# A four-layer graph network: tile-number tables loaded eight at a time, takes by node tile, four relation buffers, last-source gathers beside a linear layer

## The reference, cut to what matters

```python
h = maximum(layernorm(x), 0); x = x + L0(h)   # three GCN sums: segment_sum(norm * (h @ W)[src], dst)
h = maximum(layernorm(x), 0); x = x + L1(h)   # attention, 4 heads of 8
#   scores = einsum(q[dst], k[src]) / sqrt(8); e = exp(scores - segment_max(scores)[dst])
#   out = (segment_sum(e * v[src], dst) / segment_sum(e, dst)) @ Wo
h = maximum(layernorm(x), 0); x = x + L2(h)   # relational
#   a = tanh(relu(sum((h[src] @ A1 + b) * (h[dst] @ A2 + b + rel_emb[etype])) / sqrt(32)))
#   nei = segment_sum(a * sum_b(w_comp[etype, b] * h[src] @ weight[b]), dst)
#   curr = h[src[last edge of each node]] @ self_loop_weight; out = relu(where(degree > 0, nei + curr, 0))
h = maximum(layernorm(x), 0); x = x + L3(h)   # tensor product
#   message: source features (8 scalars, 8 vectors) times sh0 (1), sh1 (3), sh2 (5) of the edge, mixed; segment_sum by dst
```

## Time and profile before

| | us |
|---|---|
| median of 3 runs | 19102.2 (19086.82 to 19113.71) |
| profiled execution | 19072.43 |
| its span, first to last instruction | 19070.7 |
| records, path, layer 0, tables | 0 to 8208 |
| score pass | 8208 to 10774 |
| softmax, value pass | 10776 to 11757 |
| relation pass | 11935 to 15637 |
| linear layers of layer 2 | 15641 to 15948 |
| harmonic pass | 15989 to 18889 |
| last linear layer, output | 18889 to 19071 |

### The profile page before, as it was taken

The page is one execution under the profiler, slowest core; times in us unless marked ns, Lnnn a source line. Parts: engine busy times, 40 slices in busy tenths (PEclk is TensorE's granted clock), DMA queues, the critical chain, the costliest instruction groups (busy, mean ns, idle before and its releaser), DMA issues. The chain is left out here.

```text
span 19070.7 us, 197183 instructions
## 1 busy us (share of the span) xinstructions
PE 7563.1 (40%) x35336; PEld 4417.5 (23%) x35337; DVE 6411.3 (34%) x15885; ACT 2666.7 (14%) x4339; POOL 9705.1 (51%) x10318
## 2 busy tenths in 40 slices
PE   4122223444441221211111165666666655444445
PEld 1111112222221111110000032233333335322324
DVE  6222222222223333322212465455555532222222
ACT  1121223444441111100000000000000001000001
POOL 0566665555556666556666332444444442555553
PEclk9555556666665555555555555777788865666665
DMA  2111112222211111132222121222222221000001
GB/s 76 28 25 25 25 25 57 58 62 60 60 48 19 19 19 19 19 101 65 64 63 65 41 72 49 52 49 48 49 50 49 50 49 46 18 17 17 17 17 42
DMA packets 756783, 828.62 MB, mean 43 GB/s; under 512 B 348196, under 2 KB 521615, under 8 KB 753650
## 3 DMA queue, kind: packets, MB, share of 16 engines
q0 software_dynamic: 340624, 383.65, 10.8%
q1 hardware_dynamic: 251322, 306.39, 5.2%
q10 hardware_dynamic: 164008, 130.83, 2.5%
HBM read 658.54 MB, written 158.81 MB: 43 GB/s over the span
## 5 line engine op out<-in xcount | busy, mean ns | idle before, releaser
L725 POOL DMA_INDIRECT rel_ring<-scratch_tab,rel_staged x1664 | 1588.0, 954 | 2002.1 <-DVE rel_staged L714 1527.9
L725 POOL DMA_INDIRECT sh_ring<-scratch_tab,sh_staged x1664 | 1569.9, 943 | 1620.1 <-DVE sh_staged L714 1136.1
L664 PE MATMUL rel_accumulator<-rel_message,rel_onehot 128*128 128x512 f32 x3328 | 1930.2, 730 | 808.0 <-issue 488.4
L1186 POOL DMA_INDIRECT sum0g_ring<-scratch_parts,sum0g_staged x1568 | 1540.1, 982 | 1179.7 <-issue 829.7
L1186 POOL DMA_INDIRECT sum1g_ring<-scratch_parts,sum1g_staged x1568 | 1541.7, 983 | 1156.1 <-SPq L1210 653.1
L1818 POOL DMA_INDIRECT score_ring<-scratch_tab,score_staged x1664 | 1583.3, 951 | 1011.8 <-DVE score_staged L714 528.3
L1186 POOL DMA_INDIRECT sum2g_ring<-scratch_parts,sum2g_staged x1568 | 1511.4, 964 | 941.4 <-issue 463.3
L664 PE MATMUL sh_accumulator<-sh_message,sh_onehot 128*128 128x248 f32 x3328 | 1335.0, 555 | 1614.9 <-issue 1380.0
L664 PEld LDWEIGHTS sh_accumulator<-sh_message,sh_onehot 128*128 128x128 f32 x3328 | 850.4, 279 | 2098.9 <-issue 1994.3
L1859 PE MATMUL score_q_edge<-query_parts,score_onehot_t 128*128 x1664 | 422.5, 254 | 2167.5 <-issue 2105.3
L664 PEld LDWEIGHTS rel_accumulator<-rel_message,rel_onehot 128*128 128x128 f32 x3328 | 736.4, 234 | 1696.3 <-issue 1695.5
(11 more groups left out here) (423 smaller groups left out, 12703.9 us busy)
## 6 DMA issues: line engine op xcount, KB each, us to landing
score_rows<-scratch_rel_rows SPq DMA_DIRECT2D x211, 256.0 KB
rel_rel_rows<-scratch_rel_rows ACTq DMA_DIRECT2D x211, 256.0 KB
scratch_kv<-score_ring SPq DMA_DIRECT2D x208, 256.0 KB
value_ring<-scratch_kv SPq DMA_DIRECT2D x208, 256.0 KB, 2.6
rel_type_rows<-scratch_type_rows ACTq DMA_DIRECT2D x211, 172.0 KB
rel_ring<-scratch_tab,rel_staged POOLq DMA_INDIRECT x1672
score_ring<-scratch_tab,score_staged POOLq DMA_INDIRECT x1664
sh_ring<-scratch_tab,sh_staged POOLq DMA_INDIRECT x1664
```

What stands on the lines that cost most here:

```text
L664: last = self.nc.tensor.matmul(into, onehot, part, start=False, stop=True, skip_group_check=True)
L725: nc.gpsimd.indirect_dma_start(out=ring[:, q, g, :], out_offset=None, in_=table, in_offset=bass.IndirectOffsetOnAxis(ap=staged[:, q, g:g + ...
L1186: nc.gpsimd.indirect_dma_start(out=ring[:, q % slots, g, :], out_offset=None, in_=table, in_offset=bass.IndirectOffsetOnAxis(ap=staged[:, ...
```

## The change

- `merge_path` makes two byte tables by step instead of the word of odd bits and the `places` word: `tile_no` (tile number plus one) and `odd`. The word keeps the first tile and the end bits.
- `_eight` loads eight entries of a table into eight registers of TensorE with one call. `_tiles_of` and `_odd_of` use it; `_tile_registers`, `_places` and `Adder` go, and `StepAdder` takes the wait's value and the bank from the tables. The value pass has two banks instead of four and takes tiles in a loop over pairs.
- Relation pass: four buffers for look-up results (PSUM), transposed one-hots and messages; VectorE waits for adds two halves further back, and its order is messages n, staging, logits n+1, one-hots n+4; TensorE looks up half n+4. ScalarE (`_take_ends`) keeps the word, tests a half's four end bits at once and only then each step's bit, and loads the tile number where a tile ends.
- The 98 last-source gathers move to POOL beside `rlo_lin` (`beside`), and `rlo_own` runs after it.
- Harmonic pass: ScalarE only moves finished tiles, in a loop over tiles (`_move_tiles`), and issues the stores of the sums itself; SP loads the factors; VectorE copies them to PSUM, one group ahead.

```diff
+def _eight(nc, engine, table, group, low, high):
+    return nc.values_load_multi_w_load_instructions(
+        table[0:1, bass.ds(group * G, G)], engines=(engine,), min_val=low, max_val=high,
+        skip_runtime_bounds_check_because="a node tile or its place by step")[1]
+def _tiles_of(nc, k, group):
+    return _eight(nc, mybir.EngineType.PE, k["tile_no"], group, 1, JP)
+def _odd_of(nc, k, group):
+    return _eight(nc, mybir.EngineType.PE, k["odd"], group, 0, 1)
...
+class StepAdder:
...
     def add(self, g, onehot, rows):
...
+        if g % 2 == 0:
+            self.pe.wait_ge(self.cleared, self.tiles[g + 1])
+        self.nc.tensor.matmul(self.accumulator[:, bass.ds(self.odd[g] * BANK, self.width)], onehot, rows,
+                              start=False, stop=True, skip_group_check=True).then_inc(self.added, 1)
...
+def _move_tiles(nc, act, k, accumulator, taken, totals, width, cleared, added, copied, saved):
+    def move(turn, h):
+        tile = turn * 2 + h
+        end = act.value_load(k["ends"][0:1, bass.ds(tile, 1)], min_val=1, max_val=S + LEAD)
+        act.wait_ge(saved[h], turn * DMA + DMA)
+        act.wait_ge(added, end)
+        nc.scalar.copy(taken[:, h * BANK:h * BANK + width], accumulator[:, h * BANK:h * BANK + width]).then_inc(copied, 1)
         act.wait_ge(copied, tile + 1)
+        act.dma_start(totals[:, bass.ds(tile * width, width)], taken[:, h * BANK:h * BANK + width]).then_inc(saved[h], DMA)
+        nc.scalar.copy(accumulator[:, h * BANK:h * BANK + width], k["zeros"][:, 0:width]).then_inc(cleared, 1)
...
+def _take_ends(nc, act, k, word, half, step, accumulator, taken, width, cleared, added, copied, checked, saved):
+    H = G // 2
+    with act.If((word & (((1 << H) - 1) << (7 + half * H))) > 0):
+        for g in range(H):
+            with act.If((word & (1 << (7 + half * H + g))) > 0):
+                tile = act.value_load(k["tile_no"][0:1, bass.ds(step + g, 1)], min_val=1, max_val=JP) - 1
+                act.wait_ge(added, step + (g + 1 + LEAD))
...
@@ score_pass
-                        tiles = _tile_registers(nc, pe, _word(pe, k, i * R + q))
+                        tiles = _tiles_of(nc, k, i * R + q)
...
-                                                    q_nodes[:, bass.ds(tiles[g] * W, W)], start=True, stop=True)
+                                                    q_nodes[:, bass.ds(tiles[g] * W - W, W)], start=True, stop=True)
@@ value_pass
-                    words = [_places(pe, k, i * R + q) for q in range(R)]
...
-                        adder = Adder(nc, pe, BANKS, accumulator, 3 * width, cleared, added, words[q])
+                        adder = StepAdder(nc, pe, accumulator, 3 * width, cleared, added, _tiles_of(nc, k, i * R + q), _odd_of(nc, k, i * R + q))
@@ relation_pass, VectorE
-                            dve.wait_ge(added, n * H + LEAD - H)
-                            dve.wait_ge(looked_up, n + 2)
-                            if h == 1:
-                                dve.wait_ge(rowed[(m + 3) % 8 // 2], (i + (m + 3) // 8 + 1) * 2 * DMA)
-                            make_one_hots(dve, n + 3, (m + 3) % 8)
-                            if h == 1:
-                                dve.wait_ge(gathered[(q + 1) % R], (i + 1 + (q == R - 1)) * G * DMA)
-                            make_logits(dve, n + 1, m + 1, (q + h) % R, 1 - h)
+                            dve.wait_ge(added, n * H + LEAD - 3 * H)
                             make_messages(dve, n, m, q, h)
                             if h == 0:
                                 _stage(nc, k, staged, i * R + q + R - 1, (q + R - 1) % R).then_inc(indexed, 1)
+                            else:
+                                dve.wait_ge(gathered[(q + 1) % R], (i + 1 + (q == R - 1)) * G * DMA)
+                            make_logits(dve, n + 1, m + 1, (q + h) % R, 1 - h)
+                            if h == 0:
+                                dve.wait_ge(rowed[(m + 4) % 8 // 2], (i + (m + 4) // 8 + 1) * 2 * DMA)
+                            make_one_hots(dve, n + 4, (m + 4) % 8)
@@ relation_pass, TensorE
-                    words = [_word(pe, k, i * R + q) for q in range(R + 2)]
                     for q in range(R):
-                        adder = Adder(nc, pe, 2, accumulator, WIDTH, cleared, added, words[q])
+                        adder = StepAdder(nc, pe, accumulator, WIDTH, cleared, added,
+                                          _tiles_of(nc, k, i * R + q), _odd_of(nc, k, i * R + q))
+                        ahead = _tiles_of(nc, k, i * R + q + 2)
...
-                            look_up(pe, n + 3, m + 3, ahead)
+                            look_up(pe, n + 4, m + 4, ahead[h * H:(h + 1) * H])
@@ relational
+            node_linear(nc, k, "rlo_lin", dram["totals"], J, 4, w, out[:].rearrange("p j f -> p (j f)"), load=True, beside=gather_last)
             node_linear(nc, k, "rlo_own", current[:].rearrange("p j f -> p (j f)"), JP // 4, 1, own_w, flat_h)
@@ harmonic_pass, VectorE
                         _one_hot(nc, k, onehot[q % 2], (i * R + q) * G).then_inc(made, 1)
+                        dve.wait_ge(loaded[(q + 1) % R], (i + 1 + (q + 1) // R) * DMA)
+                        dve.wait_ge(messaged, i * R + q + R)
+                        spread_parts(dve, q + 1)
```

222 lines of the change are left out of this document (88 added, 134 removed).

## The result

The changed kernel takes 19548.77 us (median of 4 runs, 19504.23 to 19599.27) against 19099.11 us: ratio 1.0235, 95% interval 1.0211 to 1.0259. It is slower, where 17,400 us was forecast. The profiled execution took 19599.27 us, its span is 19597.2 us.

A forecast was written before the change was run, and what follows sets the result against it. Bound by stage: GpSimd's gathers, starving TensorE's issue, in score and harmonic passes; TensorE in relation and value passes. Score -400, value -100, relation -400, last-source gathers -50, harmonic -740, tables -10: -1700, giving 17,400 us, range 16,600 to 18,500.

The forecast's parts named there:

- What bounds the kernel: Whole kernel: the bound differs by stage; gathers starve TensorE of issue, its lateness stops the gathers, and the score pass swings.
- if a table costs about as much as one word, two cost up to 1.84 us: Value pass: two table loads partly within existing idle time, 3.3 us per group, a gain of 100 us.
- The second rival: A table costs two words, 1.84 us: value loses 420 us, relation 200; total 18,560 us; chance 18%.
- the rule beside the sum: Table loads: the Trainium skill's 200 ns per register gives 1.6 us per table, total about 18,500 us.
- Loads: Relation pass: three tables replace one and a half words per group, 1.2 us more; the shorter stream saves 1.25 us.
- The 1.85 us should go: Relation pass: four buffers and VectorE's new order remove TensorE's wait for VectorE, 1.85 us per group.
- the longer run of unbroken gathers, which deeper buffers permit, starves TensorE: Relation pass, worst case: starving as long as in the score pass, with loads on top, a loss of 80 us.
- The 1.95 us per group: Relation pass main loop: net gain per group from shorter stream, less waiting and more loads, or 400 us.
- Score pass: Look-ups 1 to 2 us apart under gathers, which hardly stop or only briefly: a gain of 400 us, ends 120 and 486.
- Both under 10 us, so the gathers set the pace: Harmonic pass: VectorE 3.8 and TensorE 8.2 us per group, below the gathers' 10: a gain of 740 us.
- the worse end of the step: Last-source gathers: 110 us gained in the tail, as much lost in the linear layer, net nothing; 50 us was taken.
- The fourth: Rival: eight registers are eight loads at 0.4 us each, so slower by 790 us, 19,890 us; chance 6%.

The follow-up runs named there:

- e9: Kernel before without the score pass's 1664 gathers, on a chip where gathers slow issue: score pass 758 us, against 2586 with gathers there.
- e11: Changed kernel with each load of eight in the value pass made by two loads of four: value pass 1234 us, relation pass 4225 us.
- e10: Changed kernel with packed words instead of tables in all passes, on a chip where gathers slow issue: 19628.97 us, ratio 1.018; relation pass 3932 us.
- e17: Changed kernel plus one wait holding the relation pass's gathers until TensorE has added groups up to N-4: 19009.06 us, ratio 0.9945; relation pass 3604 us.
- e16: Best parts together: e13's relation pass, value pass as before, harmonic pass as changed, score pass with table and held gathers: 18245.84 us, ratio 0.9559.
- e12: e8 with tables added in the score and harmonic passes alone: 18772.26 us against 19282.11, ratio 0.9739; relation pass 3607 us.
- e13: e10 plus a wait holding the relation pass's gathers until TensorE has added groups up to N-4: 18761.7 us, ratio 0.9826; relation pass 3196 us.
- e8: Kernel before with only the last-source gathers beside the linear layer and the new harmonic pass, both with words: 18959.55 us, ratio 0.9923.
- e1: Changed kernel with packed words instead of tables in all passes, on the chip where gathers slow nothing: 15386.62 us, ratio 1.0088.
- e4: e1 with the kernel before's relation pass (two buffers), on the chip where gathers slow nothing: 15333.36 us, ratio 1.0053.
- e3: Kernel before without the score pass's 1664 gathers, on the chip where gathers slow nothing: score pass 758 us, against 2082 with gathers there.
- e15: e10 with ScalarE's part of the relation pass as before, a branch for each step: ratio 1.0203; relation pass 3927 us.
- e2: Changed kernel meant to issue the value pass's loads twice, edit dropped in the build: 16,694 us against 15,252 where gathers slow nothing.

## Why the prediction was wrong, point by point

- **What bounds the kernel.** That gathers slow the issue of the other engines' instructions, and that the score pass swings because of it, was right (e9). The trace has three unlisted instructions per look-up, not four, 1.4 us each where slowed, not 1. That not every chip does this could not be seen in one trace.
- **Value pass: the price of a table.** The step "if a table costs about as much as one word, two cost up to 1.84 us" failed. A table costs 1.98 us, so two cost 4.2 us with what stands around them, and a group takes 5.5 us instead of 3.3. The other half of the step held and went further: the matmuls took 1.2 us instead of the assumed 1.6 to 2.65. The second rival, a table at 1.84 us, gave 5.3 to 6.3 us per group. I had given it 18%, though nothing in the rows bounded a load of eight by that of one; the rule beside the sum pointed the right way. A word costs 0.30 us, not up to 0.92, so a table costs more than six of them.
- **Relation pass: three steps failed.** (1) Loads: taken at 1.2 us net per group, with another 1.25 us to be saved by the shorter stream; together they are a loss of 5.5 us on the quiet chip. Where issue is slowed the loss is 1.4 us without the wait (4225 against 3932, e11 and e10) and 1.8 us with it (e17 and e16): TensorE was idle there anyway, and part of the loads seems to fall into that time. (2) "The 1.85 us should go": TensorE's idle time by VectorE's messages was 306 us after and 307 before. With words the four buffers did take it from 322 to 94 us (e12 and e10), but the idle time on issue rose from 942 to 1529 us. (3) The sentence "the longer run of unbroken gathers, which deeper buffers permit, starves TensorE", put down as the worst case with a loss of 80, is what happened: 325 us. Taking it for an end of the range rather than for what follows from my own reading of the score pass was the mistake: that reading (fast for some 5 us after a resume, then starved) says by itself that runs of two groups are worse than runs of one. e13, the opposite edit, bears it out, though it ties the gathers to TensorE's adds as well as shortening their runs. The parts add up: +325 for the buffers, +293 for the tables and -128 for the tail are 490 us, and 469 were measured. (The 1.95 us per group that the forecast took as its net gain are 1.90 by its own terms, a slip without weight.)
- **Score pass: right mechanism, mis-sized.** The look-ups came 1.4 us apart, as forecast. Left out were the unlisted instructions of the group itself, for the loop, the table and the waits: 12.3 us between two groups under gathers. Eight steps and this gap are over 20 us where issue is slowed, against 10 us of gathers, so the swing stays: 147 us instead of 400.
- **Harmonic pass.** ScalarE's loop and VectorE's copy alone gave 147 us (e8: 2902 to 2755), the tables as much again or more (2755 or 2821 to 2629 in e12). VectorE's wait for the factors went, but TensorE's matmul group is idle 1692 us in the changed kernel, 1615 before. The cause named has changed: 422 us are down to issue instead of 1380, 1264 to VectorE's messages instead of 188. VectorE waits ahead of its one-hots for TensorE's adds of two groups before. In 76 of 208 groups it began more than 3 us, up to 27 us, after even the last add of the group before is down as ended; on the quiet chip (e1) in none. So under gathers news of finished work comes late too, not only issue, and the forecast had no term for that. "Both under 10 us, so the gathers set the pace" compared times without gathers with the floor of the gathers; under them they don't hold. 298 us instead of 740.
- **Last-source gathers.** The tail lost 128 us, the linear layers gained 118 (e8): nothing is left, the worse end of the step. On the quiet chip the gain is the whole 110 us.
- **The rivals.** The total, +450 us, is near none. The second had the value pass right, but left the score and harmonic passes their forecast gains and the relation pass 200 us of loss instead of 469. The fourth ended on the right side with the wrong price: 2 us per load, not 3.2.

## What to carry to other kernels

Price a bulk load into registers by its registers, some 0.2 us each on the engine that waits for it, unless a trace shows otherwise; packing a group's small numbers into one word and shifting them out was cheaper in the value pass, which has no gathers (981 against 1148 us), and in the relation pass on either kind of chip. Where gathers slow the other engines, try to hold them back until the dependent engine has caught up: in the relation pass deeper buffers alone cost 325 us, and one wait on the gathering engine then took 731 us off. That this is a matter of short runs holds for that pass only. In the harmonic pass the change made runs of four groups out of runs of two (50, where 91 were of two), and the pass became shorter. And count the instructions of the loop around a group, not only those of its steps, when the price per instruction is what you cut.

## What the runs showed of the hardware that was not expected

- The same kernel took 15,252 us on one chip and 19,096 to 19,282 us on three others. Nearly the whole difference lies in stages with gathers: the three sums of layer 0 6214 us against 7568, score pass 2082 against 2564, relation pass with two buffers 2377 against 3580, harmonic 2098 against 2755 (e4 and e8, whose passes are alike), while the value pass (784 us in e3 and e8) and the score pass without gathers (758 us on either, e3 and e9) are equal. The same change can cost 2% on one chip and 9% on another: the changed kernel's ratio is 1.0235 on one and 16,694/15,252 = 1.095 on the quiet one. Of one chip the kernel before took 19,282 us beside e9 to e12 and 19,096 beside e13 to e15, so totals taken at different times differ by 1% there.
- Under gathers, where they slow, an operation on registers takes 0.70 us in TensorE's trace instead of about 0.04, from a median of 5.6 us after a run of gathers begins (score pass before). Semaphores are seen late too (harmonic pass, above).
- Idle time of a few microseconds for loads goes with a lower granted clock in a busy pass: 0.80 with tables against 0.92 with words on the quiet chip, and 252 us more of busy time for the same matmuls.
- A load whose registers nothing uses never reaches the program (e2), so an instruction added to measure its price has to have its result used.
